# A three-layer decoder on one core: the first group's row maxima placed among the projections' products, layer norm and values shared out anew between VectorE and ScalarE

## The reference

```python
def _forward(x, Wq, bq, Wk, bk, Wv, bv, Wo, bo, W_cross, shift_weights, gate):
    Q = (x @ Wq.T + bq).reshape(b, s, H, hd)
    K = (x @ Wk.T + bk).reshape(b, s, H, hd)
    V = (x @ Wv.T + bv).reshape(b, s, H, hd)
    ...
    scores = (gt * scores_cross + (1.0 - gt) * scores_conv) * scale
    scores = jnp.where(causal[None, None], scores, -jnp.inf)
    attn = jax.nn.softmax(scores, axis=-1)
    out = jnp.einsum('bhqk,bkhd->bqhd', attn, V).reshape(b, s, H * hd)
    return out @ Wo.T + bo
...
x = x + _L0_attn_ref(_layernorm(x, axis=-1), ...)
```

## Time and profile before

| | us |
|---|---|
| median of 3 runs | 1120.48 (1118.62 to 1124.39) |
| profiled execution | 1129.87 |
| its span, first to last instruction | 1128.1 |
| PE busy | 1045.1 (93%) |
| DVE busy | 741.7 (66%) |
| ACT busy | 562.6 (50%) |
| POOL busy | 222.3 (20%) |

### The profile page before, as it was taken

One profiled execution on the slowest core, in us unless ns is written; L12 is line 12 of the kernel. 1 busy time (PEld: TensorE's weight loads), 2 busy tenths in 40 slices (PEclk: granted clock), 3 DMA queues, 4 the chain that ended last, 5 costly groups with the idle time before them and its releaser, 6 DMA issues. The chain is left out here.

```text
span 1128.1 us, 19085 instructions
## 1 busy us (share of the span) xinstructions
PE 1045.1 (93%) x7044; PEld 620.4 (55%) x7092; DVE 741.7 (66%) x1603; ACT 562.6 (50%) x1061; POOL 222.3 (20%) x199
## 2 busy tenths in 40 slices
PE   2888889999999999999999799899898899999997
PEld 2777434444444444444444366444443688888886
DVE  5999887777787778877885266555444555555552
ACT  1445146666666667666766458377655211111110
POOL 6545540000000000000000023201101133333331
PEclk9999779999999999999999899699968899999999
DMA  8259812333444444444400135687971211111101
GB/s 245 104 198 232 260 30 40 64 67 71 74 74 79 81 77 78 81 81 78 78 16 14 25 102 138 144 197 150 220 157 64 74 39 50 51 51 49 44 20 37
DMA packets 87827, 105.27 MB, mean 93 GB/s; under 512 B 14910, under 2 KB 76010, under 8 KB 86199
## 3 DMA queue, kind: packets, MB, share of 16 engines
q1 hardware_dynamic: 85239, 100.90, 38.4%
q10 hardware_dynamic: 2496, 3.16, 1.3%
HBM read 61.80 MB, written 37.06 MB: 88 GB/s over the span
## 5 line engine op out<-in xcount | busy, mean ns | idle before, releaser
L738 DVE TENSOR_REDUCE pm<-bank 128x1 f32<-128x512 f32 (+3 forms) x608 | 356.6, 653 | 87.5 <-PE bank L814 66.7
L786 ACT ACTIVATE prob<-bank 128x512 f32<-128x512 f32 (+1 forms) x608 | 317.4, 583 | 186.0 <-PE bank L830 99.1
L809 PE MATMUL bank<-stk,stq 96*128 96x512 bf16 (+3 forms) x768 | 227.4, 340 | 5.1 <-DVE pm L738 2.9
L826 PE MATMUL bank<-stq,stk 98*128 98x512 bf16 (+3 forms) x768 | 222.4, 330 | 2.6 <-ACT prob L786 0.5
L840 PE MATMUL bank<-prob,va 128*17 128x512 f32 (+3 forms) x1536 | 145.5, 497 | 2.5
L809 PEld LDWEIGHTS bank<-stk,stq 96*128 96x128 bf16 x768 | 68.8, 98 | 136.9 <-DVE pm L738 81.0
L1541 ACT ACTIVATE e_sg<-bank 128x512 f32<-128x512 f32 x48 | 28.7, 598 | 189.3 <-PE bank L135 189.3
L959 POOL TENSOR_TENSOR c_rstd<-c_ve,mhalf 128x4 f32<-128x4 f32 x8 | 8.1, 1011 | 504.9 <-DVE c_ve L128 504.9
L1296 ACT ACTIVATE xprob<-bank 80x512 f32<-80x512 f32 x128 | 72.5, 592 | 69.1 <-PE bank L1336 67.8
L826 PEld LDWEIGHTS bank<-stq,stk 98*128 98x128 bf16 x768 | 69.4, 99 | 44.9 <-ACT prob L786 9.2
L1258 DVE TENSOR_REDUCE xpm<-bank 128x4 f32<-128x320 f32 x128 | 59.0, 488 | 39.1 <-PE bank L1321 37.5
(11 more groups left out here) (172 smaller groups left out, 1403.8 us busy)
## 6 DMA issues: line engine op xcount, KB each, us to landing
qk<-a_parts SPq DMA_DIRECT2D x32, 384.0 KB, 4.4
od<-xu SPq DMA_DIRECT2D x16, 512.0 KB, 4.8
xq<-c_parts SPq DMA_DIRECT2D x16, 384.0 KB, 2.7
xstq<-xq SPq DMA_DIRECT2D x32, 192.0 KB, 4.6
stq<-qk SPq DMA_DIRECT2D x30, 192.0 KB, 4.0
stk<-qk SPq DMA_DIRECT2D x15, 384.0 KB, 6.5
vs<-a_vst SPq DMA_DIRECT2D x8, 544.0 KB, 4.7
oall<-u_out SPq DMA_DIRECT2D x64, 64.0 KB
```

The lines of the kernel that those rows point to most:

```text
L738: nc.vector.tensor_reduce(pm[:, k, h0:h0 + hb, r], src[:, 0:hb * w].rearrange("p (h w) -> p h w", h=hb), AX, ALU.max).then_inc(s_mxe, 1)
L786: nc.scalar.activation(prob[:, U % NPS, 0:hb * n], bank[STB[U % NSB]][:, 0:hb * n], ACT.Exp).then_inc(s_ex, 1)
L809: mm = nc.tensor.matmul(dst[:, h * w:(h + 1) * w], stq[i][0:R, half, h0 + h, r * P:(r + 1) * P], stk[i][0:R, h0 + h, k0:k0 + w], start=(h ...
L826: mm = nc.tensor.matmul(dst[:, h * n:(h + 1) * n], stk[i][0:RM, h0 + h, kt * P:(kt + 1) * P], stq[i][0:RM, half, h0 + h, q0:q0 + n], start ...
```

## The change

1. Of the first group's 39 leading items, 28 (`NLEAD`) move into chunks 4 to 7 of the projections, seven per chunk, on TensorE and on VectorE (`LEAD_AT` says how many behind each of six places). They use two banks of their own (`LDB`), 6 and 7. For that the products have three banks in turn instead of four, and the values one instead of two.
2. TensorE's order in a chunk becomes: products 0, 1, transposes, first half of the values, product 2, second half of the values, product 3. The second half waits until the first is out of the bank.
3. The layer norm goes from VectorE to ACT, with POOL making the negative mean times the scale (`negm`).
4. The values leave PSUM on VectorE (first half) and ACT (second half) in chunks 0 to 3, and on ACT alone in chunks 4 to 7, without a bias. The bias is multiplied by the output weights once, behind the last chunk, and added to the output bias (`bo_b`).
5. The first two groups' loads go into chunks 2 and 3 in SP's queue, between the stores of products 1 and 2; before, they stood behind chunks 3 and 4. The third group's load goes from ACT's queue to SP's, behind the barrier. The first group's first turned maxima are written behind chunk 6.

```diff
-        TB, QKB, VB = (0, 1), (2, 3, 4, 5), (6, 7)
+        TB, QKB, VB = (0, 1), (2, 3, 4), 5
...
+                    if c in (2, 3) and n == 1:
+                        for w in range(2):
+                            sp.wait_ge(so[w], 64)
+                            sp.wait_ge(vo[w], 16)
+                        sp.wait_ge(s_set, c - 1)
+                        load_self(sp, c - 2)
...
-                if c in (3, 4):
-                    for w in range(2):
-                        sp.wait_ge(so[w], 64)
-                        sp.wait_ge(vo[w], 16)
-                    sp.wait_ge(s_set, c - 2)
-                    load_self(sp, c - 3)
+                if c == NCH - 2:
+                    self_rows(sp, 0, 0)
...
             nc.gpsimd.tensor_tensor(rstd[:, c % 2], ve[:, c % 2], mhalf[:], ALU.pow).then_inc(s_pow, 1)
+            g.wait_ge(s_pow, c + 1)
+            nc.gpsimd.tensor_tensor(negm[:, c % 2], mom[:, c % 2, 0], rstd[:, c % 2], ALU.mult).then_inc(s_nm, 1)
...
             for c in range(NCH):
+                at = LEAD_AT if c >= LEAD_FROM else (0,) * 6
                 split(c, 0)
+                for n in islice(lead, at[0]):
+                    self_item(v, 0, n)
                 split(c, 1)
+                for n in islice(lead, at[1]):
+                    self_item(v, 0, n)
+                if c + 2 < NCH:
+                    stats1(c + 2)
                 if c + 1 < NCH:
                     turned_low(c + 1)
-                if c + 2 < NCH:
-                    stats1(c + 2)
+                for n in islice(lead, at[2]):
+                    self_item(v, 0, n)
+                if c < LEAD_FROM:
+                    need(v, vo[c % 2], 16 * (c // 2))
+                    v.wait_ge(s_vm, 2 * c + 1)
...
                 split(c, 2)
+                for n in islice(lead, at[3] + at[4]):
+                    self_item(v, 0, n)
                 split(c, 3)
...
+            normalise1(1)
             for c in range(NCH):
                 need(a, so[c % 2], 64 * (c // 2))
                 high(c, 0)
...
+                middle(c, 1)
+                need(a, vo[c % 2], 16 * (c // 2))
+                if c >= LEAD_FROM:
+                    values_out(c, 0)
                 high(c, 2)
-                middle(c, 1)
+                if c + 2 < NCH:
+                    normalise1(c + 2)
+                middle(c, 2)
+                values_out(c, 1)
                 high(c, 3)
-                middle(c, 2)
                 middle(c, 3)
...
             def values(c, w):
-                need(t, s_ve, 2 * (c - 1) + w + 1)
+                need(t, s_ve, 2 * c + w)
...
+            def product(c, n):
+                need(t, s_r, 4 * c + n - 2)
...
+            for i in range(2, NB):
+                load_self(sp, i)
             for g in range(G):
-                maxima(g, 1)
+                self_rows(sp, g, 1)
...
-            g.wait_ge(s_later, 16 * 4)
+            g.wait_ge(s_bob, 1)
```

More of the change, by code:

```diff
@@ L1 @@
 from contextlib import ExitStack
+from itertools import islice
 import concourse.bass as bass
@@ L445, in qkv_scalar @@
+            v.wait_ge(s_later, 16 * 4)
+            v.wait_ge(s_bo, 1)
+            nc.vector.tensor_tensor(bo_b[:], bank[TB[0]][:, 0:D], bo_b[:], ALU.add).then_inc(s_bob, 1)
         def qkv_scalar(a):
@@ new lines, in qkv_tensor @@
+                product(c, 2)
+                for n in islice(lead, at[3]):
+                    self_maxima(t, 0, n)
+                values(c, 1)
+                for n in islice(lead, at[4]):
+                    self_maxima(t, 0, n)
+                product(c, 3)
+                for n in islice(lead, at[5]):
+                    self_maxima(t, 0, n)
+            t.wait_ge(s_xt, KT * NCH)
+            t.wait_ge(s_bvb, 1)
+            t.wait_ge(s_later, 16 * 4)
+            for k in range(KT):
+                m = nc.tensor.matmul(bank[TB[0]][:, 0:D], bvb[:, k], wo[:, k], start=(k == 0), stop=(k == KT - 1))
@@ L706, in self_sync @@
                 if g + 1 < G:
[L707 removed]
+                    self_rows(sp, g + 1, 0)
                 b = g // GB - 1
@@ new lines, in self_maxima @@
+        def self_maxima(t, g, n):
+            i, N = g % NB, g * NMX + n
+            kind, m = ring[n]
+            dst = mx_bank(N)
+            if n == 0:
+                t.wait_ge(ld[i], 16 * NLD * (g // NB + 1))
+            need(t, s_mxe, N + 1 - (len(LDB) if g == 0 else NMB))
+            if kind == "t":
+                t.wait_ge(s_mt, 2 * g + m + 1)
+                nc.tensor.transpose(dst[0:32, 0:P // 2].bitcast(BF16),
+                                    mt[:, m].rearrange("p t m -> p (t m)"), identb[:]).then_inc(s_mxf, 1)
+                return
+            half, k, r, h0, hb, k0, w, diag = mx_units[m]
+            for h in range(hb):
+                mm = nc.tensor.matmul(dst[:, h * w:(h + 1) * w],
+                                      stq[i][0:R, half, h0 + h, r * P:(r + 1) * P],
+                                      stk[i][0:R, h0 + h, k0:k0 + w],
+                                      start=(h == 0), stop=not diag, skip_group_check=True)
+            if diag:
+                mm = nc.tensor.matmul(dst[:, 0:hb * w].rearrange("p (h w) -> p h w", h=hb)[:, :, w - P:w],
+                                      identb[:], tri_q[:, 0:hb], start=False, stop=True, skip_group_check=True)
+            mm.then_inc(s_mxf, 1)
@@ L845, in self_tensor @@
             if first:
-                for n in range(NMX - 1):
-                    maxima(0, n)
+                for n in range(NLEAD, NMX - 1):
+                    self_maxima(t, 0, n)
                 return
@@ L863, in self_tensor @@
                     elif what == "r" and g + ahead < G:
-                        maxima(g + ahead, which)
+                        self_maxima(t, g + ahead, which)
             for s in range(len(sets)):
```

214 lines of the change are left out of this document (110 added, 104 removed).

## The result

The changed kernel takes **1135.03 us** (median of 4 runs, 1131.23 to 1137.49) against 1119.98 for the kernel before (4 runs, 1118.62 to 1124.39): ratio 1.0124, 95% interval 1.0084 to 1.0165. It is slower, where the forecast was 1117.5 and the range ended at 1125.0. Its profiled execution took 1135.52 with a span of 1133.4.

What follows compares the result with a forecast made beforehand. DVE was taken to pace projections and first maxima, PE to be full from the second group on. Gain 4.8 us at the first mark, less 2.3 given back, plus 0.5 for loads: 3.0 off 1120.48, so 1117.5; range 1109.5 to 1125.

Steps and rivals of the forecast that it cites:

- rival B: One half-clock dip behind PE's wait ahead of the second values in each of seven chunks, 10.9 us: 1128.4; chance 0.12.
- what is given back behind the first mark: Two DVE operations delayed by POOL's additions (2.0 us) and a late second row of maxima (0.3): 2.3 us.
- the first mark: PE's start on the first group's turned second row of maxima (L804), forecast to move from 152.26 to 147.5 us.
- The ring of chunks 0 to 3: Engines wait for each other in a circle through the values' one bank: 11.8 us per chunk, 12.7 with the stall.
- The stall: Chunks with statistics: DVE's small operations wait for POOL's low part, 0 to 1.2 us per chunk, 0.9 taken.
- The copies: Values out of PSUM, two copies: 0.8 us on ACT (0.66 to 1.0), 0.95 on DVE (0.7 to 1.0).
- Chunks 4 to 7: A longer ring through layer norm, maxima and statistics, 13.8 us; chunks forecast at 12.9, 13.8, 12.5 and 10.3 us.
- the second mark: Start of the second group's turned second row of maxima, forecast at 182.1 us against 184.63 before.
- The 0.3 for the rows: First group's second row of maxima, queued behind group 2's load on SP: 0.3 us lost (0 to 1.5).
- The loads: With earlier loads, ACT's one 4.8 us wait for stores in chunk 7 goes; 0.5 us added to the gain.
- Rival A: No meeting of DVE and POOL in the chunks: PE ends the projections 5.3 us earlier, 1112.2; chance 0.35.
- Rival C: First group's load lands 3 us late for chunk 4 and PE stands still for 3: 1120.5; chance 0.08.

Runs made afterwards that it cites:

- a_fill: Changed kernel plus 13 matmuls whose result nobody reads, filling PE's wait ahead of the second values in chunks 0 to 3: 1126.09 us, ratio 1.0025.
- the 12-run ratio: The changed kernel once more, unaltered, 12 runs against the kernel before: 1131.63 us, ratio 1.0058 (1.0024 to 1.0092).
- a_no_lead: Changed kernel without maxima among the products (all 39 behind the projections), POOL's additions held back: 1147.80 us, ratio 1.0205.
- r4: Changed kernel with two value banks (chunks 0-3), statistics, power and high half moved ahead, POOL's additions and ACT's value copies later, units re-placed: 1110.33 us, ratio 0.9889.
- o8_again: Changed kernel in the earlier order and banks, maxima behind projections, with statistics, power and high half of turned x moved ahead: 1127.60 us, ratio 0.9974.

## Why the prediction was wrong

The prediction said no difference, and the change is slower. The step that failed is the sum for chunks 0 to 3: it put the second values and product 3 at their full-clock 1.42 and 1.43 us behind a wait that the change creates, so the lower clock was priced at nothing there and left to rival B with a chance of 0.12. It cost 6.9 us. A second term was too small: what is given back behind the first mark, 2.3 forecast and 4.5 measured.

**The ring of chunks 0 to 3** was right in its links (second values, three products, high part, split, statistics, low halves, copies) and in its length: 12.7 forecast, 12.8 with PE's wait filled. **The stall** of 0.9 was right: 1.06 to 1.15 for an operation of 0.17. It is what is left of POOL's instruction (0.58 in the earlier trace rows, 0.53 once in a_fill), so "1.2 whenever they meet" is its upper end. **The copies** were mis-sized: ACT's two took 1.07 to 1.10, above the upper bound of 1.0, DVE's two 1.05 instead of 0.95, its bound also 1.0. The ring's length came out right all the same (its terms as listed add up to 11.86, and 12.8 with the stall). **Chunks 4 to 7**: 12.9, 13.8, 12.5 and 10.3 forecast; 12.1, 13.6, 12.2 and 10.6 measured.

**The clock.** The sum held 1.42 and 1.43 us for the second values and product 3, lengths taken from a loop in which PE hardly waited, and put them behind a wait that the change itself creates, of 3.2 to 3.4 us in each of the chunks 0 to 3. They cost 1.3, 2.3, 1.8 and 1.5 us more in chunks 0 to 3 (chunk lengths of the change less those with the wait filled): 6.9 of the 9.0 us by which the trace missed the forecast at the second mark. B priced a dip at 1.55 us, close to the mean of 1.7. What spoke against it, a clock of 0.96 over the loop before, is an average over a loop without a wait of that length. B also read "one pair" at half clock; the loop before has four waits of 1.96 to 1.99 us ahead of the transposes, and behind two of them the products took 4.58 and 4.59 us, behind the other two 3.03 and 3.02. The later two:

```profile
93.92 1.09 PE L513 MATMUL bank<-ident,a_xn 128*128 128x128 f32 x8 [1.98 <-DVE a_xn L355]
94.77 3.02 PE L135 MATMUL bank<-a_xnt,wk 128*128 128x512 f32 x12
...
105.42 1.09 PE L513 MATMUL bank<-ident,a_xn 128*128 128x128 f32 x8 [1.99 <-DVE a_xn L355]
106.26 4.59 PE L135 MATMUL bank<-a_xnt,wk 128*128 128x512 f32 x12
```

So a dip was already an even chance at 2 us, and the change made the wait 3.2 to 3.4. B was counted over seven chunks; it came in the four that have the wait. Half of B is 1123.0, not the 1125 at which the range ends. The clock's 6.9 us alone would have given 1124.4, still inside; with the 2.2 us more given back and the loads' 0.5 it is 1127.1, which is the 12-run ratio of 1.0058 on the prediction's base.

**Given back.** 2.3 us forecast, 4.5 measured between the marks (5.4 in the second trace). The meeting with POOL's additions was found in the right place, but I let the three banks hide half of it. PE waited 3.0 us just ahead of the turn, for DVE's reductions behind the two operations, and ran at clock 0.73 from 169.6 to 176.0; with the additions moved the whole 4.7 us went. The 0.3 for the rows was 0.6.

**The loads.** 0.5 forecast, nothing measured.

**The rest of the 1.2%** is not settled by a mechanism. The marks carry 6.5 to 8.5 us (either trace of the change against either of before, at mark 2), the 12-run ratio 0.6%; the same text of before differed from itself by 1.1% in one four-run median, with its time lost behind the second mark. I hold the change to be 0.6% slower.

**Rival A** (no meeting of DVE and POOL) didn't happen. **Rival C** (load late) neither: the first unit of chunk 4 stood for nothing in the change.

## What to carry to other kernels

A wait of PE that a change creates can have two prices, its own length and the lower clock for what stands behind it. Here half clock would have cost the 2.85 us of work behind each wait another 2.85, and 1.3 to 2.3 were measured; if that work is on the ring, put such a term into the sum, or fill the wait. When a step moves to another engine, look for the latest of its inputs and for what stands behind it in the new queue, not only for busy time: here the layer norm on ACT won nothing until DVE's statistics, POOL's power and ACT's copy of the turned x were all moved ahead, and then chunks 1 to 3 ran at PE's pace. And when a ring opens, ask what it had been holding back: at 9.3 us per chunk the DMA share reached 1.03 to 1.15, and ACT waited for stores.

## What had not been expected

- Work that nobody reads brought the kernel forward: 13 matmuls, 3.2 us in each of four chunks, moved the first mark 6.9 us ahead, and the last 7.0.
- With two banks, waits of 2.21 and 2.24 us in two chunks were followed by pairs of products of 3.22 and 4.62 us (2.96 without a wait): nearly the same wait, once with next to no price and once with 1.7 us. After the waits of 3.2 to 3.4 us there was a price each time, also in the six of a_no_lead.
- DVE's small operation ended within 0.03 us of POOL's wherever it began behind POOL's start (three traces), and took 0.16 where it began 0.03 us ahead of it.
- The DMA share of a stretch can read above 1 (1.03 to 1.15); in and behind such stretches ACT waited 2.3 to 6.2 us for stores to land (r4, o8_again).
